# A linear attention and quantised ffn layer on one core: the DMA queue's order and three engines' orders laid out anew, and a first turn that prepares the ffn weight later

## The reference

```
h   = layernorm(x)
q   = elu(h Wq' + bq) + 1;  k = elu(h Wk' + bk) + 1;  v = h Wv' + bv      # 16 heads of 32
num = q . cumsum(k (x) v);  den = max(q . cumsum(k), 1e-6)                # over tokens
x   = x + layernorm((num / den) Wo' + bo)
y   = layernorm(x), in blocks of 32 features scaled and rounded to FP6 e2m3 values
x   = x + layernorm(y wd' + bias)       # wd: the ffn weight, rounded the same way
```

## Time and profile before

| | |
|---|---|
| median of 3 runs | 2397.03 us (2395.23 to 2401.79) |
| the profiled execution | 2399.21 us |
| its span, first to last instruction | 2397.4 us |
| mean granted TensorE clock | 0.993 of full |
| TensorE busy | 2332.0 us, 97% |
| DVE busy | 1984.1 us, 83% |
| GpSimd busy | 1470.3 us, 61% |
| ScalarE busy | 1080.8 us, 45% |
| data the DMA queue moves | 191.47 MB, 24.5% of 16 engines' span |

### The profile page before, as it was taken

One profiled execution on the slowest core, in us unless ns is written; L12 is line 12 of the kernel. 1 busy time (PEld: TensorE's weight loads), 2 busy tenths in 40 slices (PEclk: granted clock), 3 DMA queues, 4 the chain that ended last, 5 costly groups with the idle time before them and its releaser, 6 DMA issues.

```text
span 2397.4 us, 63827 instructions
## 1 busy us (share of the span) xinstructions
PE 2332.0 (97%) x26146; PEld 1905.0 (79%) x26146; DVE 1984.1 (83%) x3988; ACT 1080.8 (45%) x1840; POOL 1470.3 (61%) x1730
## 2 busy tenths in 40 slices
PE   7999999999999999999999999999999999999997
PEld 5877888888788788888787887888878888878785
DVE  7888889888788888898888887888988888878886
ACT  4444444444444444444444444444444444444442
POOL 2566566666566665666665665656666656656554
PEclk9999999999999999999999999999999999999999
DMA  4222221222222322222322222222123222223211
GB/s 158 71 92 98 75 77 62 88 99 73 86 65 75 99 90 80 77 65 86 99 73 90 73 71 91 96 76 75 62 89 99 73 90 73 71 91 95 77 46 37
DMA packets 108227, 195.55 MB, mean 82 GB/s; under 512 B 15136, under 2 KB 21664, under 8 KB 107424
## 3 DMA queue, kind: packets, MB, share of 16 engines
q1 hardware_dynamic: 107936, 191.47, 24.5%
HBM read 155.65 MB, written 35.78 MB: 80 GB/s over the span
## 4 chain that ended last, share of the span: by engine, by line
PE 79%; DMA 7%; DVE 4%; ACT 3%; issue 3%; POOL 2%; SPq 2%; POOLq 0%; DVEq 0%; ACTq 0%
PE work L423 12%; PE work L425 11%; PE work L424 11%; PE score L423 10%; PE score L424 10%; PE score L425 10%; PE work L540 5%; PE work L442 4%; PE score L505 4%; DMA rden_dram<-rinv 3%; DMA kc<-rden_dram 3%; PE state_bank L553 1%; POOL f_buf L1425 1%; DVE A L1020 1%; PE score L527 1%
## 5 line engine op out<-in xcount | busy, mean ns | idle before, releaser
L1020 DVE TENSOR_TENSOR A<-score,causal 128x512 f32<-128x512 f32 x512 | 329.2, 681 | 21.5 <-PE score L505 21.5
L1395 POOL TENSOR_TENSOR exp_t<-exp_t,x_coef 128x512 f32<-128x512 f32 x124 | 198.5, 1601 | 148.6 <-DMA exp_t<-in_xt 148.6
L725 ACT CAST oT_hi<-kc 128x512 fp32r<-128x512 f32 x128 | 79.6, 622 | 365.4 <-DVE kc L1015 365.4
L1402 POOL TENSOR_TENSOR x_res<-x_res,o_buf 128x512 f32<-128x512 f32 x128 | 175.6, 1372 | 104.5 <-ACT o_buf L670 104.5
L423 PE MATMUL work<-wo_hi,oT_hi 128*128 128x512 f32 x512 | 204.2, 399 | 14.8 <-ACT Kn L720 11.9
L423 PE MATMUL work<-wv_hi,xT_hi 128*128 128x512 f32 x512 | 214.9, 420 | 0.0
L423 PE MATMUL score<-xT_hi,wq_hi 128*128 128x512 f32 x512 | 208.1, 406 | 6.8 <-DVE KT L960 6.8
L1397 POOL TENSOR_TENSOR exp_t<-exp_t,x_coef 128x512 f32<-128x512 f32 x124 | 205.2, 1655 | 9.7
L423 PE MATMUL score<-xT_hi,wk_hi 128*128 128x512 f32 x512 | 205.7, 402 | 0.0
L425 PE MATMUL work<-wv_hi,xT_lo 128*128 128x512 f32 x512 | 202.2, 395 | 0.6 <-issue 0.6
L424 PE MATMUL work<-wv_lo,xT_hi 128*128 128x512 f32 x512 | 201.8, 394 | 0.9 <-issue 0.9
(11 more groups left out here) (134 smaller groups left out, 6393.1 us busy)
## 6 DMA issues: line engine op xcount, KB each, us to landing
x_in<-in_x SPq DMA_DIRECT2D x128, 256.0 KB, 4.3
x_res<-in_x SPq DMA_DIRECT2D x128, 256.0 KB, 2.8
kc<-rden_dram SPq DMA_DIRECT2D x128, 256.0 KB
exp_t<-in_xt SPq DMA_DIRECT2D x124, 256.0 KB, 3.1
out<-f_buf SPq DMA_DIRECT2D x96, 256.0 KB, 2.0
x_coef<-coef_dram SPq DMA_DIRECT2D x31, 512.0 KB, 3.8
out<-xd SPq DMA_DIRECT2D x32, 256.0 KB, 2.1
rden_dram<-rinv SPq DMA_DIRECT2D x32, 64.0 KB, 3.5
```

The costliest lines, as they stand in the source:

```text
L1020: nc.vector.tensor_tensor(A[:, j, :, :], score_bank[j][:], causal[:].unsqueeze(1).to_broadcast([P, G, P]), ALU.mult).then_inc(a_set, 1)
L1395: nc.gpsimd.tensor_tensor(rows, rows, by_token(0), ALU.mult).then_inc(x_scaled, 1)
L1402: nc.gpsimd.tensor_tensor(x_res[:, b, :], x_res[:, b, :], o_buf[:, b % 2, :], ALU.add).then_inc(r_set, 1)
```

## The change

What it does:
- **DMA queue.** `load_x` runs two tiles ahead (`after = i + 2 < TILES`), tile 1's loads are issued before turn 0. `load_xt` 0 and 1 stay ahead of `store_rden`, but output 1's store goes behind `spread_rden(i, 0)`, `load_xt` 2 ahead of `spread_rden(i, 2)`, `load_xt` 3 ahead of `spread_rden(i, 3)`, and the loads of x_res go late, those of b = 1 to 3 to the end.
- **ScalarE, DVE and GpSimd** have new orders in every turn but the last. TensorE's steady order is as before.
- **First turn.** Wo is staged in x_res instead of kc, its `high` and `low` come late (`low("o")` between `clamp` and `invert`), Wv is loaded second, the last multiplication of `quantise_wf` goes to GpSimd (`dequantise_wf`), and the transposes of the ffn weight go behind q(3) and v(0), in other banks.

The diff, cut to its core:

```diff
-                 "o": kc[:].rearrange("p g b t -> p (g b t)")[:, 0:G * D].rearrange("p (g d) -> p g d", g=G)}
+                 "o": x_res[:]}
-        W_DONE = {"k": G, "q": G + 1, "o": G + 2, "v": G + 3}
+        W_DONE = {"k": G, "q": G + 1, "v": G + 2, "o": G + 3}
-        wf_bank = [work[0], work[1]]
+        wf_bank = [work[2], work[1], work[2], work[0]]
@@ DMA queue, load_res
+                else:
+                    sp.wait_ge(w_lo_set, W_DONE["o"])
@@ DMA queue, turn (the new order whole)
+                after = i + 2 < TILES
                 store(i - 1, 0)
+                load_x(i + 2, 0), load_x(i + 2, 1)
                 store_coef(i + 1), spread_coef(i + 1)
+                load_x(i + 2, 2)
                 load_xt(i + 1, 0), load_xt(i + 1, 1)
                 store_rden(i), spread_rden(i, 0)
                 store(i - 1, 1)
                 spread_rden(i, 1)
                 load_xt(i + 1, 2)
                 spread_rden(i, 2)
                 store(i - 1, 2)
                 load_res(i, 0)
                 load_xt(i + 1, 3)
                 spread_rden(i, 3)
                 store(i - 1, 3)
+                load_x(i + 2, 3)
                 load_res(i, 1), load_res(i, 2), load_res(i, 3)
@@ TensorE, first turn
                 q(2)
                 q(3)
                 wf_transposes(0), wf_transposes(1)
                 ...
                 v(0)
                 wf_transposes(2), wf_transposes(3)
                 scores(0)
@@ ScalarE, turn, from the past copies (the new order; before: f_norm(1), past, seed(0), kn(0), o_hi(0), seed(1), x_hi(i+1,0), f_norm(2), kn(1), x_hi(i+1,1), o_hi(1), o_norm(0), kn(2), seed(2), f_norm(3), x_hi(i+1,2), o_hi(2), kn(3), seed(3), ...)
+                past(0..3), f_norm(1), seed(0), x_hi(i + 1, 0), kn(0), kn(1), o_hi(0),
+                f_norm(2), seed(1), o_hi(1), x_hi(i + 1, 1), f_norm(3), o_norm(i, 0),
+                kn(2), seed(2), seed(3), o_hi(2), x_hi(i + 1, 2), kn(3), x_hi(i + 1, 3),
+                r_norm(i, 0), o_norm(i, 1), o_hi(3), state()
@@ DVE, turn, from clamp (the new order)
+                clamp(), invert(), v_bias(0), f_seen(2), join(f, 2), mask(0, 0), mask(0, 1),
+                widen(f, 2), mask(0, 2), mask(0, 3), f_bias(3), x_lo(i + 1, 0), f_seen(3),
+                mask(1, 0), normalise(0), mask(1, 1), o_lo(0), mask(1, 2), mask(1, 3), ...
@@ DVE, turn, its start: x_seen(i+1, b) spread out, phi_k(0) ahead of greatest(i - 1, 1)
@@ DVE, first turn
                 quantise_wf()                    # without its last multiplication
                 low("q")
-                phi_k(0), low("o"), phi_k(1), x_seen(1, 0), x_seen(1, 1), scan(0), ...
+                x_seen(1, 0), x_seen(1, 1), phi_k(0), join, phi_k(1), widen, low("v"),
+                phi_k(2), phi_k(3), scan(0), ...
+                clamp(), low("o"), invert(), v_bias(0), wf_low(2), wf_low(3), mask(0, 0), ...
@@ GpSimd, turn
                 product(0)
+                rstd(i + 1, "x", 3)
                 product(1)
                 ...
                 output(1), x_scale(i + 1, 0), x_scale(i + 1, 1), rstd(f, 2), output(2), ...
                 residual(i, 0), x_scale(i + 1, 2), output(3), x_scale(i + 1, 3), ...
+            def dequantise_wf():                 # first in the first turn
+                pool.wait_ge(wf_quantised, 2)
+                pool.wait_ge(w8_set, 1)
+                nc.gpsimd.tensor_tensor(A, q8, xs to_broadcast, ALU.mult).then_inc(wf_quantised, 1)
```

More of the change, by code:

```diff
@@ L366, in turn @@
                     spread_coef(i + 1)
[L367 to L370, removed]
+                if after:
+                    load_x(i + 2, 2)
                 if nxt:
@@ L410, in _ @@
                 load(dst[:], src.to_broadcast([P, D]), small_loaded)
+            for b in range(NSEQ):
+                load_x(1, b)
             turn(0, False, True, True)
@@ L479, in v @@
                         take(pe, i, ("v", b), here, before)
+                        if first and b == 0:
+                            pe.wait_ge(wf_lo_set, 2)
                         weights(i, "v")
@@ L734, in seed @@
                     if cur:
+                        if first and b == 0:
+                            act.wait_ge(wf_lo_set, 3)
                         take(act, i, ("att", b), {0} if first else {-1, 0}, set())
@@ L1219, in turn @@
                     x_seen(i + 1, 0)
+                phi_k(0)
+                if nxt:
+                    join(i + 1, "x", 0)
                     x_seen(i + 1, 1)
-                    x_seen(i + 1, 2)
-                    join(i + 1, "x", 0)
                 greatest(i - 1, 1)
+                scale(i - 1, 1)
                 if nxt:
                     widen(i + 1, "x", 0)
-                scale(i - 1, 1)
+                quantise(i - 1, 1)
+                xd_lo(0)
+                o_bias(i - 1, 3)
@@ L1227, in turn @@
+                if nxt:
+                    x_seen(i + 1, 2)
+                o_seen(i - 1, 3)
+                r_seen(i - 1, 2)
+                join(i - 1, "o", 3)
+                phi_k(1)
+                widen(i - 1, "o", 3)
+                if nxt:
+                    x_seen(i + 1, 3)
+                join(i - 1, "r", 2)
+                scan(0)
+                f_bias(0)
+                scan(1)
                 if nxt:
                     join(i + 1, "x", 1)
-                quantise(i - 1, 1)
+                widen(i - 1, "r", 2)
@@ L1230, in turn @@
+                f_seen(0)
+                if nxt:
+                    widen(i + 1, "x", 1)
+                phi_k(2)
+                join(i - 1, "f", 0)
+                r_seen(i - 1, 3)
+                scan(2)
+                widen(i - 1, "f", 0)
+                join(i - 1, "r", 3)
                 if nxt:
                     join(i + 1, "x", 2)
-                o_bias(i - 1, 3)
-                xd_lo(0)
-                o_seen(i - 1, 3)
-                phi_k(0)
-                join(i - 1, "o", 3)
@@ L1295, in turn @@
                 f_bias(3)
-                normalise(0)
-                o_lo(0)
+                if nxt:
+                    x_lo(i + 1, 0)
                 f_seen(3)
                 mask(1, 0)
+                normalise(0)
                 mask(1, 1)
+                o_lo(0)
+                mask(1, 2)
+                mask(1, 3)
                 join(i - 1, "f", 3)
                 v_bias(1)
-                mask(1, 2)
-                mask(1, 3)
                 o_bias(i, 0)
```

299 lines of the change are left out of this document (143 added, 156 removed).

## The result

The changed kernel takes 2433.31 us (median of 4 runs, 2429.54 to 2441.38) where the kernel before took 2398.03 beside it: a ratio of 1.0147, with an interval of 1.0126 to 1.0167. It is slower; 2374 was forecast. The profiled execution took 2430.87 us with a span of 2429.1, 31.7 more than before.

What follows compares the result with a forecast made beforehand. TensorE, busy 97%, was taken to bound the kernel, so only its idle time could be won. 22 + 4.5 - 3 = 23.5 us off 2399.2 gave 2375.7, forecast as 2374 for the runs' median; range 2362 to 2392.

Steps and rivals of the forecast that it cites:

- (a): DMA queue, steady turns: output 1's store goes behind store_rden and spread 0; copies start about T+24.6; with (b) 22 us won.
- (b): ScalarE, steady turns: kn(1) moves ahead of o_hi(0), so waits for Kn and masks go; with (a) 22 us won.
- (c): ScalarE, steady turns: x_hi(0) ahead of kn(0), f_norm(1) behind the past copies; missed margins charged 3 us, ends 0 and 9.
- kn(0): ScalarE, steady turns: forecast to end at T+28.2, before state(0) wants it at T+28.6, with 0.4 us to spare.
- rival 3: x_hi(0) holds kn(0) on ScalarE and TensorE stands at state(0): 30 turns make 45 us, 2419; chance 7%.
- (d): DMA queue: x loaded two turns ahead, x_res and exp_t 2 and 3 later; hidden, worth 0.
- (e): TensorE's issue waits ahead of the denominators' products: 9.9 us stays, term 0, ends -10 and +20.
- rival 1: Refills get slower where DMA and small matmuls meet: five turns become like turn 8, +20 us, 2394; chance 15%.
- The first turn: Turn 0: weight work moved or reordered so TensorE's early waits shrink; 4.5 us won, ends 2 and 7.
- Rival 2: The wait only changes its name: o_lo(0) and masks replace Kn, only the first turn is won, 2392 us; chance 7%.
- Slower: The sign that the whole kernel loses time: chance 0.09, from rival 3 and the far end of rival 1.

Runs made afterwards that it cites:

- the first experiment: Changed kernel with normalise(3) and o_lo(3) moved ahead of scale(0)/quantise(0) and quantise(0)/o_bias(2) on DVE in steady turns: 2399.61 us, ratio 0.9992.
- Experiments 2 and 3: 2: changed kernel with GpSimd's output(3) back behind rstd(r, 0), 2438.54 us. 3: kernel before with only the DMA queue's new order, 2599.45 us.
- experiment 4: Kernel before with the change's first turn on every engine, its own steady turns kept from turn 1 on: 2393.93 us, ratio 0.997.
- experiments 1 and 5: 1: the first experiment. 5: its kernel with x_coef's round trip moved ahead of the store of output 0: 2375.92 us, ratio 0.9907.

## Why the prediction was wrong

**(a), right.** Loads of exp_t at T+16.6, as forecast; copies by T+23.4 where T+24.6 was forecast.

**(b), right.** No wait for Kn or masks is left in the steady turns; the stretches are 23 us shorter, 22 was forecast.

**(c), the step that failed.** The prediction walked o_lo(0), kn(0), kn(2) and the masks, found them 0.3 to 0.6 us early, and charged "0.1 us a turn, 3 us" for all margins together. The walk stops at attention product 2. o_lo(3), which o(3) of the next turn wants, is not on the list, and it alone costs 57.0 us, 1.90 a turn. Neither end of the term, 0 to 9, came near. It could have been found in the trace of before: o_lo(3) ended 0.15 us ahead of o(3) in turn 14, and step (b) was about to bring o(3) more than a microsecond nearer. With nothing in the diff that made o_lo(3) earlier, and one instruction of 1.3 us (output 3) put into its chain, the wait was due. The rest is size: quantise(0) at 1.62 instead of 0.68 us and the shift at 1.21 instead of 0.72 make 1.4 of the 1.76 us of turn 11. A walk with the lengths of turn 14 would have given a wait of some 0.3 us a turn, 10 us in all (an estimate, for this arm of the chain alone), and the sign would still have been missed. Without the stretches at o(3) the profiled execution would stand at 2430.9 - 57.0 = 2373.9 us, where the sum has 2375.7; but that is a subtraction and no kernel, as the first experiment shows with 2399.6.

**kn(0), right (rival 3 wrong).** kn(0) ends at T+27.9, forecast T+28.2; state(0) starts at 949.37 (T+28.6) with no wait.

**(d), right with its condition.** GpSimd does not wait for x_res in the steady turns. Experiments 2 and 3 show how near that is: 92 and 235 us of such waits when one instruction or the whole order is put back.

**(e), right for this kernel and wrong as a rule.** The issue stretches cost 2.7 us more, 0 was taken. But without the wait at o(3) they cost 20.4 more again, above the +20 of the term's end if the two are put together. The prediction had the place (rival 1) and took the amount from turns in which x_coef ran alone. Of the 4.4 us by which its turn 8 is longer than turn 16, 2.69 is the stop and the rest is the clock, which is at half from 642.6 us on for 3.4 us; the prediction priced the two as one. That five turns should become like turn 8 was the wrong picture: the turns that have a boundary there are fixed by the count of instructions; what the traffic bears on is the cost of each. The small matmuls there are 160 in the trace (128 and 32), not 192.

The Trainium skill, "Runtime: NRT & Kernel Launch", section "Instruction fetch mechanics", states blocks of 256 instructions; the shift of 13 matmuls in two turns and the experiments with 13 increments agree. That crossing a block is mostly hidden holds here where large matmuls are among the 256 instructions ahead, and not where nearly all are small: 0.2 to 4.2 us for each such crossing. Had the rule held throughout, the 13 increments would have won nothing.

**The first turn, right in sum.** q(0) 1.05 us earlier (0.9 forecast), past products at 44.40 (45.2), attention product 0 at 55.69 (56.9), q(0) of turn 1 5.4 earlier (4.5); alone it is worth 5 us (experiment 4). A stall of 2.33 is left before the past products.

**The range.** Added up at their ends, the terms give about 2365 to 2389 without (e) and 2355 to 2409 with it, which is wider than the 2366 to 2383 that the sum states; 2433 lies outside all of these.

**Rivals.** Rival 2 had the right sentence, the wait changes its name, for the wrong instruction and with the wrong price: it let the new wait cost as much as the old one won, while a wait in every turn costs what it costs. Among the things that "would be wrong", the row of TensorE waiting for oT_lo was named; it had no price and no chance of its own. Slower had 0.09, all of it for x_hi(0) and the far end of rival 1.

## What to carry to other kernels

When a wait is taken away, everything that the same engine does later comes due earlier by that much: list every operand of the rest of the turn and of the next turn's first products with its margin in the old trace, above all the one with the smallest (here 0.15 us). Add the length of what the change puts into its chain, and take for that chain the longer of the durations that the trace has: the same DVE instruction took 0.68 us in one order and 1.62 in another. On an engine that is busy 97%, the price of a wait depends on what else stands around it, so a wait that is mended can show less than its own length (issue stretches 24.6 us in the changed kernel, 45 with o(3) mended, almost none with 13 idle instructions a turn). Look at the granted clock around each stop: a part of its price can stand there as slower matmuls and in no row of waits.

## What was not expected of the hardware

- In the kernels before and after and in those of experiments 1 and 5, TensorE stops at a 256th instruction whenever it went through the 256 ahead of it in less than 2.7 us, and at some where this took up to 4.4: ten to twelve stops in 30 turns, 0.2 to 4.2 us each, always at the place that the count gives. 13 increments a turn, which mix large matmuls into those 256, took 35 us off one kernel (ratio 0.9992 to 0.9847), 22 off another (1.0147 to 1.0053), and nothing off a third (the kernel before), where other waits grew and four stops of 1.0 to 1.1 us came.
- The packet with the next instructions can come late when data moves, and in nearly all of these stops the next matmul runs 2.2 to 2.8 us behind its start: it starts at T+17.8 in turn 4 of the kernel before, just ahead of the data (stall 0.78 us), and at T+20.1 in the same turn of the first experiment's kernel, where the DMA engines run at some 210 to 340 GB/s (3.14 us).
- A stop can cost more than its length: at stops of 1.97 to 4.24 us the granted clock fell to 1.2 GHz for 3.4 or 6.8 us in several turns, and 30.7 us of such stretches stand in the first experiment's kernel; other stops, one of 3.47 us among them, had no such stretch.
- The same instruction has two lengths. DVE's quantise(0) takes 0.68 us in turn 14 of before and 1.62 beside GpSimd's residual(1) in turn 11 of after; a root's shift of 128x1 on GpSimd takes 0.27 or 1.21. The Trainium skill, "GPSIMD Engine Reference", lists SBUF interfaces that GpSimd shares with VectorE; both rows agree with that, but no run here varied it by itself.
